# Selective-scan and expert kernel: decay rows built from three bf16 parts of transposed running sums instead of fp32 matmuls

## What is computed

```python
a = dtc * A
cum = jnp.cumsum(a, axis=2)
cumT = cum.transpose(0, 1, 3, 2)
diff = cumT[..., :, None] - cumT[..., None, :]
mask = jnp.tril(jnp.ones((CHUNK, CHUNK), bool))
decay = jnp.where(mask, jnp.exp(jnp.where(mask, diff, 0.0)), 0.0)
...
scores = jnp.einsum('bclhg,bcshg->bchls', Cc, Bc) * decay * dtT[:, :, :, None, :]
```

## Time and profile before

| quantity | value |
|---|---|
| median of 3 runs | 2977.33 us |
| profiled execution, its own time | 2979.97 us |
| its span, first to last instruction | 2978.3 us |
| mean granted TensorE clock | 0.982 of full |
| busy: PE / weight loads / DVE / ACT / POOL | 2761.3 / 2276.2 / 2529.3 / 1724.8 / 1917.9 us |
| chain that ended last, by engine | PE 39%, DVE 32%, issue 12%, POOL 10%, ACT 6% |

### The profile page before, as it was taken

One profiled execution on the slowest core, in us unless ns is written; L12 is line 12 of the kernel. 1 busy time (PEld: TensorE's weight loads), 2 busy tenths in 40 slices (PEclk: granted clock), 3 DMA queues, 4 the chain that ended last, 5 costly groups with the idle time before them and its releaser, 6 DMA issues.

```text
span 2978.3 us, 50716 instructions
## 1 busy us (share of the span) xinstructions
PE 2761.3 (93%) x15168; PEld 2276.2 (76%) x15168; DVE 2529.3 (85%) x6406; ACT 1724.8 (58%) x3560; POOL 1917.9 (64%) x2328
## 2 busy tenths in 40 slices
PE   5899999999999999999999999999999999999985
PEld 4777887787877787887777777778777878777863
DVE  4598888988888988888988888988889888888985
ACT  4465665665565655665665666555556555665642
POOL 2276666676667676666676666666666766675755
PEclk9999999999999999999999999999999999999998
DMA  3000000000000000000000000000000000000000
GB/s 127 8 8 12 5 11 7 11 11 11 7 7 7 11 11 11 4 10 7 11 11 11 4 11 7 11 11 11 4 7 11 11 11 11 4 7 11 8 4 7
DMA packets 28183, 34.24 MB, mean 11 GB/s; under 512 B 2672, under 2 KB 27248, under 8 KB 27440
## 3 DMA queue, kind: packets, MB, share of 16 engines
q1 hardware_dynamic: 28144, 33.77, 3.5%
HBM read 25.37 MB, written 8.39 MB: 11 GB/s over the span
## 4 chain that ended last, share of the span: by engine, by line
PE 39%; DVE 32%; issue 12%; POOL 10%; ACT 6%; DVEq 1%; DMA 0%; ACTq 0%; SPq 0%; POOLq 0%
PE bank L1336 13%; DVE acc L1003 11%; POOL Em L531 8%; PE bank L1551 4%; PE bank L1516 4%; PE bank L1492 4%; PE bank L1468 3%; DVE Em L1163 3%; PE bank L1355 3%; PE bank L1543 2%; DVE Em L1172 2%; DVE acc L993 2%; DVE v L1069 2%; PE products L1501 1%; ACT acc L690 1%
## 5 line engine op out<-in xcount | busy, mean ns | idle before, releaser
L1003 DVE SCALAR_TENSOR_TENSOR acc<-bank,cw,acc 128x253 f32<-128x253 f32 (+2 forms) x1920 | 773.7, 470 | 0.0
L1336 PE MATMUL bank<-hT,w_in 128*128 128x256 f32 x2560 | 608.3, 383 | 13.0 <-DVE acc L1003 12.3
L1336 PEld LDWEIGHTS bank<-hT,w_in 128*128 128x128 f32 x2560 | 484.7, 192 | 119.7 <-issue 44.5
L531 POOL TENSOR_TENSOR Em<-ee 128x1024 f32<-128x1024 f32 x256 | 513.4, 2026 | 46.8 <-issue 46.5
L1163 DVE SCALAR_TENSOR_TENSOR Em<-Em,p 128x1024 f32<-128x1024 f32 x256 | 435.0, 1699 | 0.0
L546 POOL TENSOR_TENSOR W<-W,Em 128x1024 f32<-128x1024 f32 x128 | 336.1, 2626 | 8.5 <-ACT Em L818 0.3
L818 ACT ACTIVATE Em<-Em,rden 128x1024 f32<-128x1024 f32 x256 | 291.4, 1142 | 73.5 <-DVE Em L1172 73.5
L690 ACT ACTIVATE acc<-bank,cb,cw 128x256 f32<-128x256 f32 x640 | 325.6, 562 | 0.0
L1172 DVE TENSOR_TENSOR Em<-Em,products 128x1024 f32<-128x1024 f32 x256 | 311.1, 1215 | 4.5
L671 ACT ACTIVATE xbcT<-acc 128x512 f32<-128x512 f32 x320 | 200.3, 626 | 140.4 <-DVE acc L1003 140.3
L1501 PE MATMUL products<-w_de,h2T 128*128 128x512 f32 x512 | 235.0, 602 | 23.8 <-DVE Em L1172 23.8
(11 more groups left out here) (177 smaller groups left out, 5594.1 us busy)
## 6 DMA issues: line engine op xcount, KB each, us to landing
x_in<-x_dram SPq DMA_DIRECT2D x32, 256.0 KB, 2.7
x_res<-x_dram SPq DMA_DIRECT2D x32, 256.0 KB, 2.7
out_dram<-f SPq DMA_DIRECT2D x32, 256.0 KB, 2.2
w_in<-in_wT_dram SPq DMA_DIRECT2D x1, 3080.0 KB, 12.9
w_up<-upT_dram SPq DMA_DIRECT2D x1, 1024.0 KB, 15.5
w_de<-down_eT_dram SPq DMA_DIRECT2D x1, 1024.0 KB, 17.5
w_down<-downT_dram SPq DMA_DIRECT2D x1, 1024.0 KB, 19.5
w_ue<-up_e_dram SPq DMA_DIRECT2D x1, 1024.0 KB, 21.6
```

What stands on the lines that cost most here:

```text
L531: nc.gpsimd.tensor_tensor(Em[:, k], bc(ee[:, k, 0:XD], 2, KEYS), bc(ee[:, k, XD:XD + KEYS], 1, XD), ALU.mult).then_inc(E_done.sem, 1)
L1003: ins = V.scalar_tensor_tensor(acc[:, r, a, ahead:], ps[:, a * TOK:(a + 1) * TOK - ahead], cw[:, t, k:k + 1], acc[:, r, a, ahead:], ALU.mu ...
L1336: last = mm(ring[j % 2][:, a * TOK:(a + 1) * TOK], w_in[:, k, at:at + P], hT[:, k, :], start=k == 0, stop=k == DK - 1)
```

## The change

The rows are no longer summed up in `mixer_rows`. The running sums are computed once per group in transposed form (16 rows of tokens' sums), split into three bf16 parts whose sum is the fp32 value, and `mixer_rows` only picks one head's row out of the parts with bf16 matmuls against a constant `pick` of ones at three places of the contraction axis. For this `da` is stored four times side by side (64 of 128 columns, the rest zero, so that each copy begins at a multiple of 32), PE makes one more fp32 matmul 128x128, ACT one more copy, and POOL six operations on 128x128. No step is put in another place. The lines below are the diff without setup of semaphores.

```diff
-        da = sb("da", [P, CH, HEADS])
+        da = sb("da", [P, 4, 2 * CH * HEADS])
+        cumT = sb("cumT", [P, P])
+        cum_rest = sb("cum_rest", [P, P])
+        cum_parts = sb("cum_parts", [P, P], BF16)
+        minus_a = sb("minus_a", [P, 1])
+        minus_b = sb("minus_b", [P, 1])
+        pick = sb("pick", [P, CH * HEADS], BF16)
...
+            for first, minus in ((64, minus_a), (96, minus_b)):
+                nc.gpsimd.affine_select(out=minus[:], in_=minus[:], compare_op=ALU.is_ge, fill=0.0,
+                                       base=-first, pattern=[[0, 1]], channel_multiplier=1)\
+                    .then_inc(own_pool, own.one())
+            for block in range(3):
+                pool.wait_ge(own_pool, own.n)
+                nc.gpsimd.affine_select(out=pick[:], in_=pick[:], compare_op=ALU.not_equal, fill=1.0,
+                                       base=-32 * (block + 1), pattern=[[-1, CH * HEADS]], channel_multiplier=1)\
+                    .then_inc(own_pool, own.one())
...
-                nc.gpsimd.tensor_tensor(da[:], dts[:], bc(neg_a[:], 1, CH), ALU.mult).then_inc(da_done.sem, 1)
+                nc.gpsimd.tensor_tensor(dta[:], dts[:], bc(neg_a[:], 1, CH), ALU.mult).then_inc(own_pool, own.one())
+                pool.wait_ge(own_pool, own.n)
+                nc.gpsimd.tensor_copy(da[:, :, 0:CH * HEADS], bc(dta[:].rearrange("p c h -> p (c h)"), 1, 4))\
+                    .then_inc(da_done.sem, 1)
...
+            def mixer_parts(g):
+
+                if later(g):
+                    pool.wait_ge(rows_ps.sem, rows_ps.at(g - 1, 2 * CH - 1))
+                pool.sem_inc(arrived_pool, 1)
+                nc.gpsimd.tensor_copy(cum_parts[:], cumT[:]).then_inc(own_pool, own.one())
+                pool.wait_ge(own_pool, own.n)
+                nc.gpsimd.tensor_scalar(cum_rest[:], cum_parts[:], minus_a[:, 0:1], None, ALU.mult)\
+                    .then_inc(own_pool, own.one())
+                pool.wait_ge(own_pool, own.n)
+                nc.gpsimd.tensor_tensor(cum_rest[:], cum_rest[:], cumT[:], ALU.add).then_inc(own_pool, own.one())
+                pool.wait_ge(own_pool, own.n)
+                nc.gpsimd.tensor_copy(cum_parts[:], cum_rest[:]).then_inc(own_pool, own.one())
+                pool.wait_ge(own_pool, own.n)
+                nc.gpsimd.tensor_scalar(cumT[:], cum_parts[:], minus_b[:, 0:1], None, ALU.mult)\
+                    .then_inc(own_pool, own.one())
+                pool.wait_ge(own_pool, own.n)
+                nc.gpsimd.tensor_tensor(cum_parts[:], cum_rest[:], cumT[:], ALU.add).then_inc(parts_done.sem, 1)
...
                     mixer_cum(g)
+                    mixer_parts(g)
...
+                    act.wait_ge(parts_done.sem, parts_done.at(g - 1))
                 nc.scalar.activation(cum[:, 0:3:2],
-                                     yb[:, 0:2 * CH * HEADS].rearrange("p (a c h) -> p a c h", a=2, c=CH), ACT.Copy)\
-                    .then_inc(cum_sb.sem, 1)
+                                     yb[:, 0:2 * CH * HEADS].rearrange("p (a c h) -> p a c h", a=2, c=CH), ACT.Copy)
+                nc.scalar.activation(cumT[:], yb[:, P:2 * P], ACT.Copy).then_inc(cum_sb.sem, 1)
...
-                mm(yb[:, 0:n], tri[:], da[:].rearrange("p c h -> p (c h)"), start=True, stop=True)
-                mm(yb[:, n:2 * n], ones[:], da[:].rearrange("p c h -> p (c h)"), start=True, stop=True)\
+                mm(yb[:, 0:n], tri[:], da[:, 0, 0:n], start=True, stop=True)
+                mm(yb[:, n:2 * n], ones[:], da[:, 0, 0:n], start=True, stop=True)
+                mm(yb[:, P:2 * P], da[:].rearrange("p a b -> p (a b)"), tri[:], start=True, stop=True)\
                     .then_inc(cum_ps.sem, 1)
...
+                if c == 0:
+                    pe.wait_ge(parts_done.sem, parts_done.at(g))
...
-                        last = mm(pairb[q][:, i * P:(i + 1) * P], da[:, c, h:h + 1].to_broadcast([P, P]), tri[:],
+                        k = c * HEADS + h
+                        last = mm(pairb[q][:, i * P:(i + 1) * P], pick[:, k:k + 1].to_broadcast([P, P]), cum_parts[:],
                                   start=False, stop=i == 3)
```

More of the change, by code:

```diff
@@ L235, in sandwich @@
         dt_ps, dt_sb, dt_abs, dte_done, da_done = (sig(n) for n in ("dt_ps", "dt_sb", "dt_abs", "dte_done", "da_done"))
+        parts_done = sig("parts_done")
         cum_ps, cum_sb, cum_diff, ecum_done = (sig(n) for n in ("cum_ps", "cum_sb", "cum_diff", "ecum_done"))
@@ L332, in _ @@
             nc.gpsimd.memset(H[:], 0.0).then_inc(own_pool, own.one())
+            nc.gpsimd.memset(da[:], 0.0).then_inc(own_pool, own.one())
+            nc.gpsimd.memset(pick[:], 0.0).then_inc(own_pool, own.one())
+            nc.gpsimd.memset(minus_a[:], -1.0).then_inc(own_pool, own.one())
+            nc.gpsimd.memset(minus_b[:], -1.0).then_inc(own_pool, own.one())
             nc.gpsimd.memset(minus1[:], -1.0).then_inc(own_pool, own.one())
```

## The result

The changed kernel takes **3158.05 us** (median of 4 runs, 3155.94 to 3159.14) against 2976.64 for the kernel before (4 runs, 2972.32 to 2981.53): ratio 1.0608, 95% interval 1.059 to 1.0626. The forecast was 3065 with a range up to 3100: the sign was right, the size half of what came.

What follows compares the result with a forecast made beforehand. Bound: a chain handing over between PE, DVE and POOL, not TensorE alone. 29 x (89.0 + 0.22 + 1.5) plus 25 x 2.4 gave 2691 against 2602.65 for the steady rounds, +88: 3065 us; 8-in-10 range 2968 to 3100.

Steps and rivals of the forecast that it cites:

- third matmul: PE's added fp32 matmul of 128 columns at the running sums: two passes, counting in full, +0.22 us a round.
- mask overtaken by POOL: Chunk 1: POOL's product starts 0.1 us before DVE's mask of head 1, delaying sL by 2.0 us; +1.5 a round.
- clock: TensorE's clock halves around a 5.2 us pause before sL x Xdt: 25 of 29 rounds, 2.4 us each, 60 together.
- the size of a fall: Each clock fall at the sL x Xdt pause costs 2.4 us; bounds 0 and 2.85 in every round.
- If it falls within the pause, part costs nothing: A clock fall starting inside the pause before sL x Xdt was priced at 2.4 us instead of 2.85.
- How often: Clock falls at the pause before sL x Xdt: 25 of 29 steady rounds, against eight of twenty-eight before.
- clz: DVE's clz product, after chunk 0's earlier sL, falls into POOL's second product; rsf and all DVE behind: +0.3 us.
- the 0.5 that the prediction let the round absorb: Of PE's 2.0 us lateness at sL x Xdt, 0.5 does not reach the round's end, leaving +1.5.
- Bf16 rows: PE's row matmuls: 0.055 us each, a four-row block 0.22 instead of 0.88; none of the 2.6 saved is gained directly.
- The hidden work: ACT's copy (0.27 us) and POOL's six operations (2.2 to 2.5 us) lie in waits and cost nothing.
- Rival (2): DVE's mask stays first, pause 3.2 to 3.5 us, clock falls in most rounds: +61, 3038 us; chance 0.20.
- Rival (5): Faster: DVE's mask goes first and the clock never falls: 2970, 2962 or 2953 us; chance 0.14.

Runs made afterwards that it cites:

- e1_pad: Changed kernel with three zero matmuls of 512 columns added in each block of rows, making PE's rows as long as before: 3032.93 us, ratio 1.0135 to the kernel before.
- e2_work_alone: Changed kernel with all the added work, but the rows come from the fp32 matmuls as before: 3033.95 us, ratio 1.0132 to the kernel before.
- e4_fill: Changed kernel with 20 zero matmuls filling the pause before sL x Xdt of chunk 1, POOL still overtaking the mask: 3000.98 us, ratio 1.0026.
- e3_guard: Changed kernel in which POOL's first product of chunk 1 waits for DVE's mask of head 1: 3079.95 us, ratio 1.0298 to the kernel before.
- e10_dense_behind: Changed kernel with eight zero matmuls of 512 columns in the middle of the sL x Xdt block, behind the pause: 3124.01 us, ratio 1.0449.
- e5_guard_fill: Changed kernel with POOL waiting for DVE's mask of head 1 and twelve zero matmuls in the pause: 2949.96 us, ratio 0.9875 to the kernel before.
- e6_before_fill: Kernel before the change with six zero matmuls in its pause of 1.33 us: 2960.43 us, ratio 0.9912 to the kernel before.
- e12_pair8: Changed kernel with POOL's wait and twelve fillers, plus running sums and ninth pair ahead of the expert output's first half: 2909.09 us, ratio 0.9724.

## Why the prediction was wrong in size

The steady rounds add up as follows, beside the terms of the sum on record:

| term, us a round | forecast | measured | from |
|---|---|---|---|
| third matmul | 0.22 | 0.22 | e1_pad, e2_work_alone against 89.0 |
| mask overtaken by POOL | 1.5 | 1.04 | e4_fill against those two |
| clock | 2.4 in 25 of 29 | 5.3 in all 29 | changed kernel against e4_fill |

29 x (0.22 + 1.04 + 5.3) = 190, less 8 x 2.85 = 23 for the falls of before, is 167; the two stretches differ by 168.

- **The step that failed is the size of a fall.** The prediction took the fall of before, 6.8 us long and worth at most 2.85, and set 2.85 in every round as its upper bound. That price belonged to a fall that starts 2.1 us behind a pause of 1.33 us. This one starts 2.2 us into a pause of 4.70, has 2.5 us of idle time and 11.1 us of work at half the clock, about 5.5 lost, of which 5.3 arrive. e3_guard shows that, with this work behind the pause, the falls which begin inside it are the long ones; e10_dense_behind shows that other work behind it shortens them. "If it falls within the pause, part costs nothing" went the wrong way: it cost more. So the range was too narrow above. Its upper end should have been half the clock through all that stands behind the pause: by the earlier trace rows, from L1449 at 1426.58 to the second half of L1468 at 1433.76 it is 7.2 us, which such a fall could have doubled.
- **How often.** 25 of 29 was forecast, 29 came. At the 2.4 us forecast for each, four falls more are 10 us of the 80 that the sum lacked: the count was a small error, the length the large one. The Trainium skill ("TensorE: Matmul & The Clock Gate", What's actually happening) says that activity releases the throttle. It was the better guide to the count, and the traces agree: no steady round of e4_fill, with its pause filled, has a fall.
- **Overtaking.** Place, direction and margin (0.1 forecast, 0.18 measured) were right, and e3_guard and e4_fill confirm the mechanism. The size was too large, 1.5 for 1.04, by way of a pause of 5.2 for 4.70. The mask waited 1.5 us, not 1.7, and the 0.3 at clz did not come, so sL was late by 1.5 and not 2.0; less the 0.5 that the prediction let the round absorb, that is the 1.0 measured. The Trainium skill ("SBUF — State Buffer", SBUF: two separate sides) says that whichever of the two starts first holds the shared port pair for its whole instruction. The rows agree: 2.79 with POOL first, 1.28 with DVE first, and nothing in between at this place.
- **clz.** It was stalled as forecast, 1.48 for 0.30, but the +0.3 behind it did not appear: DVE's f, which waits 2.31 us for POOL in both kernels, begins 17.50 us into the round, and 17.56 before.
- **Bf16 rows.** Four take 0.22, as assumed, and nothing of the saving was gained directly, as forecast. The groups' 219 ns for one include the last end and are no price for a start.
- **The hidden work.** ACT's copy and POOL's operations cost nothing, as forecast, since e2_work_alone's 89.23 leaves room for the third matmul alone. POOL's six took about 3 us instead of 2.2 to 2.5: two of them, with a scalar by partition, take 0.6 each. POOL's wait for DVE's statistics is 264.4/32 = 8.3 us, 9 by the forecast and 11.5 before.
- **The rivals.** Rival (2), DVE first, is e3_guard. Its pause of 3.19 us is nearly the 3.2 to 3.5 of the rival, but its ratio of 1.0298, about 3065 us where the kernel before takes 2976.64, is more than the 3038 worked out, for the same reason as in the sum. Rival (5) needed a pause that does no harm; e5_guard_fill makes that with its fillers, and the gain is real: 1.25% below the kernel before, of which e6_before_fill shows some 0.9 to belong to the clock alone.

## What to carry to other kernels

A saving on PE ahead of a wait that it doesn't move becomes idle time, and idle time can cost more than the work saved: look at the instructions behind the pause, and price them at half the clock (here 11 us of work, in every round). Check which engine is first at each place where DVE and POOL meet: here 0.18 us decided 1.0 us a round, and one semaphore wait put it right. Cheap fillers in the pause are a quick test of whether the clock is the loss; after that the saved time can be collected.

## What the runs showed of the hardware

- With the same pause of 4.70 us, the clock stayed at 1.2 GHz for 13.65 us where 64-column fp32 matmuls and transposes followed, and for 6.8 or 3.4 where eight matmuls of 512 bf16 columns stood among them. In every kernel traced here the falls of the steady rounds lasted 3.4, 6.8, 10.2 or 13.7 us.
- At an unchanged pause of 1.33 us, falls came in 8 of 29 rounds in the trace of before (about 12 on two other chips, by an estimate), in 16 with 0.2 us more of PE in the round and in 24 with the change's added work. An idle time of 1.89 us behind six fillers gave one in the traced execution and, by the same way of estimating, five or six in two others. What decides whether a pause costs the clock was not settled.
- With zero matmuls in the pause the clock stayed at 2.4 GHz: no steady round of e4_fill, e5_guard_fill, e6_before_fill or e12_pair8 has a fall.
